# Attention values: the values stand in TensorE, placed by DMA, with repeated denominator columns, and a new step table

## What is computed

```python
q, k, v = heads(xn @ Wq.T + bq), heads(ctx @ Wk.T + bk), heads(ctx @ Wv.T + bv)
scores  = (q @ k.T * tau + delta) / sqrt(8)          # 512 x 77 for each head
x = x + softmax(scores) @ v -> merged heads @ Wo.T + bo
```

## Time and profile before

| | us |
|---|---|
| median of 3 runs | 204.74 (204.21 to 206.11) |
| profiled execution | 205.09 |
| span of its instructions | 203.3 |
| mean granted TensorE clock | 0.973 |
| busy: TensorE, VectorE, ScalarE, GpSimd | 174.1, 124.9, 90.3, 59.9 |

### The profile page before, as it was taken

The page is one execution under the profiler, slowest core; times in us unless marked ns, Lnnn a source line. Parts: engine busy times, 40 slices in busy tenths (PEclk is TensorE's granted clock), DMA queues, the critical chain, the costliest instruction groups (busy, mean ns, idle before and its releaser), DMA issues.

```text
span 203.3 us, 3835 instructions
## 1 busy us (share of the span) xinstructions
PE 174.1 (86%) x1176; PEld 142.2 (70%) x1177; DVE 124.9 (61%) x386; ACT 90.3 (44%) x216; POOL 59.9 (29%) x73
## 2 busy tenths in 40 slices
PE   7796899989999969598999999889688989989940
PEld 2435778979949945483896779765477979989930
DVE  2799967598743786984265975355478454544420
ACT  5490466344551443322239164151265557555620
POOL 8873030001305250020020002034205645646441
PEclk9998899999999996999999999999999999999996
DMA  6999980000000000000000000002801281100000
GB/s 207 289 334 380 487 365 29 0 0 3 2 0 3 0 0 0 2 3 0 0 0 3 0 0 0 3 28 79 261 32 54 74 266 31 31 6 9 27 14 2
DMA packets 9219, 15.37 MB, mean 76 GB/s; under 512 B 1578, under 2 KB 6069, under 8 KB 9136
## 3 DMA queue, kind: packets, MB, share of 16 engines
q1 hardware_dynamic: 7680, 13.00, 18.5%
q0 software_dynamic: 1088, 1.60, 2.4%
q10 hardware_dynamic: 432, 0.53, 0.8%
HBM read 13.53 MB, written 5.44 MB: 93 GB/s over the span
## 4 chain that ended last, share of the span: by engine, by line
PE 59%; DVE 24%; issue 5%; ACT 5%; POOL 2%; DMA 2%; DVEq 0%; ACTq 0%; POOLq 0%
PE scores L1108 12%; PE acc L1001 11%; PE acc L1119 8%; PE shared L957 4%; DVE QG L721 4%; PE shared L1062 4%; PE scores L982 3%; PE shared L937 3%; DVE stats L662 3%; PE shared L1048 3%; DVE XN L680 2%; PE shared L930 2%; PE shared L909 2%; DMA X<-in_x 2%; PE shared L1035 2%
## 5 line engine op out<-in xcount | busy, mean ns | idle before, releaser
L1001 PE MATMUL acc<-VP,P 123*128 123x128 f32 (+1 forms) x320 | 41.8, 276 | 0.6 <-ACT P L598 0.6
L1001 PEld LDWEIGHTS acc<-VP,P 123*128 123x128 f32 (+1 forms) x320 | 39.8, 191 | 2.8 <-ACT P L598 1.0
L598 ACT ACTIVATE P<-scores 123x512 f32<-123x512 f32 (+1 forms) x40 | 22.9, 595 | 26.3 <-PE scores L982 23.5
L638 ACT ACTIVATE HT<-scores,B 128x128 f32<-128x128 f32 x88 | 25.4, 376 | 14.3 <-PE scores L1108 10.4
L731 DVE TENSOR_REDUCE MR<-shared 128x4 f32<-128x308 f32 x64 | 26.9, 469 | 2.2 <-PE shared L957 2.0
L506 POOL TENSOR_TENSOR X<-X,ROWS 128x512 f32<-128x512 f32 x6 | 7.7, 1275 | 65.9 <-DVE XN L680 65.8
L520 POOL DMA_INDIRECT out<-XS,token x22 | 21.6, 982 | 18.2 <-DVE XS L867 10.6
L1108 PE MATMUL scores<-XST,HT 128*128 128x128 f32 x176 | 24.1, 280 | 3.3 <-ACT XST L631 2.7
L1108 PEld LDWEIGHTS scores<-XST,HT 128*128 128x128 f32 x176 | 21.4, 192 | 5.0 <-ACT XST L631 3.6
L1119 PE MATMUL acc<-W,HT 128*128 x176 | 23.2, 276 | 1.1 <-ACT HT L638 1.1
L957 PE MATMUL shared<-KG,QG 98*128 98x308 f32 x64 | 20.5, 376 | 4.3 <-DVE QG L721 3.4
(11 more groups left out here) (123 smaller groups left out, 252.0 us busy)
## 6 DMA issues: line engine op xcount, KB each, us to landing
W<-in_w SPq DMA_DIRECT2D x16, 256.0 KB, 8.6
slots<-in_empty SPq DMA_DIRECT2D x1, 2860.0 KB, 15.6
XS<-slots SPq DMA_DIRECT2D x2, 650.0 KB, 6.2
XS<-slots SPq DMA_DIRECT2D x2, 390.0 KB, 3.9
W<-in_ffn0w SPq DMA_DIRECT2D x1, 534.0 KB, 8.9
XS<-slots SPq DMA_DIRECT2D x2, 260.0 KB, 2.9
X<-in_x SPq DMA_DIRECT2D x2, 256.0 KB, 5.1
B<-in_b SPq DMA_DIRECT2D x1, 512.0 KB, 7.3
```

Source lines behind the costliest of these rows:

```text
L598: act.activation(P[0:w, n % NP], scores[n % 2][0:w, :], ACT.Exp).then_inc(probs_ready, 1)
L638: ins = act.activation(HG1[:, t % NHB, c], hidden[t % 2][:, c], ACT.Gelu_apprx_tanh, bias=B1[:, bass.ds(expert[t] * NF + k, 1)])
L1001: ins = pe.matmul(acc[qt // 2][:, c:c + VW], P[0:w, n % NP, 128 * qt:128 * qt + 128], VP[0:w, l, b, j, half], start=(t == 0 and qt % 2 == ...
```

## The change

The values are projected once for each layer, for both batches (`vp/0`, `vp/1`: two products of 77 x 128), and VectorE adds their bias while it copies them to a new tile `VS`. SyncE then copies them by DMA into `VP`, which GpSimd has set to zero before: for each batch 12 transfers (`HEADS`), one for each piece of a head's 77 rows that lies in one tile, of 15 to 77 rows with two times 8 columns. In `VP` the 64 value columns of a half stand in front of 64 columns of ones, where the mask is repeated 8 times for each head, so the denominators come out once for every value column.

In `pv` the values stand in TensorE and the 512 columns of probabilities stream through in one product; the result is transposed already, and each half has its own `acc` bank. The new step `rd` makes the reciprocal of the denominators on ScalarE as exp(-ln(d)), and `on` is one VectorE product for each half, straight into `OT`. The `ot` steps, their transposes and the 8 filler products in the last `ot` and `wo` are gone. The context is stored once. On SyncE's queue the first placing stands before the weights of layer 1's attention and of the first feed-forward part, the second before the rest of the weights. The table of steps is another one.

```diff
-VC = DK + 1
-VW = 128
+VW = 2 * HALF * DK
...
+HEADS = [(h, j, max(h * KEYS, STARTS[j]) - STARTS[j], max(h * KEYS, STARTS[j]) - h * KEYS,
+          min((h + 1) * KEYS, STARTS[j] + WIDTHS[j]) - max(h * KEYS, STARTS[j]))
+         for h in range(HALF) for j in range(NT)
+         if max(h * KEYS, STARTS[j]) < min((h + 1) * KEYS, STARTS[j] + WIDTHS[j])]
...
+R_BV = R_SB + E
+R_N = R_BV + 2 * D
...
-        one/1/1 pv/0/1/8 km/1/0 xt/2/0 pre/2/0 km/1/1 pv/0/1/9 on/0/1 q/1/0/0 max/1/0/0:2 ot/0/1 max/1/0/2:4 vp/1/1/1
...
+        ln/0/0 xn/0/0 kp/0 vp/0 xt/0/0 ks/0 q/0/0/0:2 km/0/0 max/0/0/0:6 one/0 max/0/0/6:8 ln/0/1 mt/0/0/0
+        max/0/0/8:11 sc/0/0/0:2 max/0/0/11 pre/0/0 max/0/0/12 xn/0/1 pv/0/0/0 max/0/0/13 pv/0/0/1 xt/0/1 sc/0/0/2
+        max/0/0/14:16 sc/0/0/3 q/0/1/0 mt/0/0/1 pv/0/0/2 sc/0/0/4 pv/0/0/3 q/0/1/1 pv/0/0/4 sc/0/0/5 km/0/1 sc/0/0/6
+        max/0/1/0:3 sc/0/0/7 pv/0/0/5 sc/0/0/8 max/0/1/3:6 pv/0/0/6 rd/0/0/0 max/0/1/6 sc/0/0/9 max/0/1/7 pv/0/0/7:9
+        on/0/0/0 pv/0/0/9 rd/0/0/1 mt/0/1/0 vp/1 pre/0/1 max/0/1/8 on/0/0/1 max/0/1/9:11 sc/0/1/0:2 max/0/1/11 wo/0/0
+        sc/0/1/2 ln/1/0 max/0/1/12:14 pv/0/1/0 xn/1/0 pv/0/1/1 sc/0/1/3 pv/0/1/2 max/0/1/14:16 sc/0/1/4 xt/1/0
+        pv/0/1/3 one/1 mt/0/1/1 gate/0 kp/1 sc/0/1/5 pv/0/1/4 rd/0/1/0 ut/0 pre/1/0 hid/0/0:4 sc/0/1/6 out/0 sc/0/1/7
+        pv/0/1/5 sc/0/1/8 ln/2/0 on/0/1/0 xn/2/0 sc/0/1/9 pv/0/1/6:8 ks/1 xt/2/0 q/1/0/0 pv/0/1/8:10 km/1/0
+        max/1/0/0:3 pre/2/0 max/1/0/3:5 rd/0/1/1 max/1/0/5 on/0/1/1 max/1/0/6:8 q/1/0/1 mt/1/0/0 wo/0/1 max/1/0/8
+        sc/1/0/0 km/1/1 ln/1/1 max/1/0/9 pv/1/0/0 xn/1/1 sc/1/0/1 max/1/0/10 sc/1/0/2 xt/1/1 max/1/0/11 sc/1/0/3
+        max/1/0/12:14 gate/1 pv/1/0/1:3 max/1/0/14 ut/1 max/1/0/15 sc/1/0/4 pre/1/1 hid/1/0:4 mt/1/0/1 out/1 sc/1/0/5
+        pv/1/0/3 sc/1/0/6 ln/2/1 pv/1/0/4 rd/1/0/0 xn/2/1 on/1/0/0 sc/1/0/7 pv/1/0/5 xt/2/1 sc/1/0/8 q/1/1/0:2
+        pv/1/0/6 sc/1/0/9 max/1/1/0 pv/1/0/7 max/1/1/1 pv/1/0/8 max/1/1/2:6 pv/1/0/9 max/1/1/6:11 rd/1/0/1 mt/1/1/0
+        on/1/0/1 max/1/1/11:14 sc/1/1/0:2 wo/1/0 sc/1/1/2 max/1/1/14 pre/2/1 max/1/1/15 pv/1/1/0 ln/3/0 pv/1/1/1
+        mt/1/1/1 sc/1/1/3 pv/1/1/2 sc/1/1/4:6 pv/1/1/3 sc/1/1/6 xn/3/0 xt/3/0 pv/1/1/4 route/0 sc/1/1/7:9 rd/1/1/0
+        pv/1/1/5 prob/0 rank/0 pv/1/1/6 tiles/0 sc/1/1/9 pv/1/1/7:9 on/1/1/0 pv/1/1/9 rd/1/1/1 on/1/1/1 wo/1/1 ln/3/1
+        xn/3/1 moe/-1 xt/3/1 moe/0 route/1 moe/1 prob/1 rank/1 tiles/1
...
+            def place_values(l):
+                sp.wait_ge(v_ready, l + 1)
+                sp.wait_ge(zeroed, 6 + l)
+                for b in range(B):
+                    for h, j, r, k, n in HEADS:
+                        o = VP[r:r + n, l, b, j, :, h * DK:(h + 1) * DK]
+                        v = VS[k:k + n, l, b].rearrange("p (s d) -> p s d", s=2)[:, :, h * DK:(h + 1) * DK]
+                        sp.dma_start(o, v).then_inc(v_placed[l][b], 16)
...
+            place_values(0)
+            sp.dma_start(ATT[1][:, :], att1).then_inc(in_att[1], 16)
             sp.dma_start(W0[:, :], ffn0w).then_inc(in_w0, 16)
             for i in range(3):
                 sp.dma_start(LB[32 * i:32 * i + 32, :], loraB).then_inc(in_lb, 16)
-            sp.dma_start(ATT[1][:, :], att1).then_inc(in_att[1], 16)
+            place_values(1)
...
-            finish(pool.memset(VP[:, :, :, :, :, HALF * VC:], 0.0), zeroed)
+            finish(pool.memset(VP[:, 0], 0.0), zeroed)
...
-            def ones_columns(l, b):
-                for half in range(2):
-                    o = VP[:, l, b, :, half, 0:HALF * VC].rearrange("p j (h c) -> p j h c", c=VC)[:, :, :, DK]
-                    finish(pool.tensor_copy(o, vm), ones_col)
+            def ones_columns(l):
+                m = vm.unsqueeze(3).to_broadcast([TW, NT, HALF, DK])
+                for b in range(B):
+                    for half in range(2):
+                        o = VP[:, l, b, :, half, HALF * DK:].rearrange("p j (h c) -> p j h c", c=DK)
+                        finish(pool.tensor_copy(o, m), ones_col)
...
+            finish(pool.memset(VP[:, 1], 0.0), zeroed)
...
-                    if n == 2 * B * 2 * NT - 1:
+                elif kind == "rd":
+                    _, l, b, half = s
+                    n = 2 * l + b
+                    act.wait_ge(probs_used, NT * (2 * n + half + 1))
+                    if n > 0:
+                        act.wait_ge(on_ready, 2 * (n - 1) + half + 1)
+                    act.activation(rden[:, half], acc[half][HALF * DK:, :], ACT.Ln).then_inc(act_chain, 1)
+                    chain += 1
+                    act.wait_ge(act_chain, chain)
+                    act.activation(rden[:, half], rden[:, half], ACT.Exp, scale=-1.0).then_inc(rden_ready, 1)
+                    if s[1:] == (1, B - 1, 1):
                         act.preload_act_table_set("gelu_apprx_tanh_and_others")
-                elif kind == "ot":
-                    _, l, b = s
-                    read(act, s)
-                    act.activation(OT[:, b], bank(s)[:, :], ACT.Identity, bias=ATT[l][:, A_BV:A_BV + 1]).then_inc(ot_ready, 1)
...
-                    _, l, b, j = s
+                    l = s[1]
                     read(dve, s)
-                    if (l, b, j) == (0, 0, 0):
-                        dve.wait_ge(in_con, 16)
-                    w = WIDTHS[j]
-                    o = VP[0:w, l, b, j, :, 0:HALF * VC].rearrange("p s (h c) -> p s h c", c=VC)[:, :, :, 0:DK]
-                    v = bank(s)[0:w, 0:D].rearrange("p (s h c) -> p s h c", s=2, c=DK)
-                    m = CON[0:w, C_VM + HALF * j:C_VM + HALF * (j + 1)].unsqueeze(1).unsqueeze(3).to_broadcast([w, 2, HALF, DK])
-                    dve.tensor_tensor(o, v, m, ALU.mult).then_inc(v_ready, 1)
+                    dve.wait_ge(in_rows, 16)
+                    bv = ROWS[0:KEYS, R_BV + D * l:R_BV + D * (l + 1)].unsqueeze(1).to_broadcast([KEYS, B, D])
+                    dve.tensor_tensor(VS[:, l], bank(s)[0:KEYS, 0:B * D].rearrange("p (b d) -> p b d", b=B), bv,
+                                      ALU.add).then_inc(v_ready, 1)
...
-                    _, l, b = s
-                    n = 2 * l + b
-                    dve.wait_ge(probs_used, 2 * NT * (n + 1))
-                    for i in range(2):
-                        o = acc[i][:, 0:4 * HALF * VC].rearrange("p (t h c) -> p t h c", t=2, c=VC)
-                        ins = dve.reciprocal(rden[:, b, 2 * i:2 * i + 2], o[:, :, :, DK])
-                    link(ins)
-                    for i in range(2):
-                        o = acc[i][:, 0:4 * HALF * VC].rearrange("p (t h c) -> p t h c", t=2, c=VC)
-                        rd = rden[:, b, 2 * i:2 * i + 2].unsqueeze(3).to_broadcast([128, 2, H, DK])
-                        dve.tensor_tensor(ON[:, b, 2 * i:2 * i + 2].rearrange("p t (h c) -> p t h c", c=DK),
-                                          o[:, :, :, 0:DK], rd, ALU.mult).then_inc(on_ready, 1)
+                    _, l, b, half = s
+                    dve.wait_ge(rden_ready, 2 * (2 * l + b) + half + 1)
+                    dve.tensor_tensor(OT[64 * half:64 * half + 64, b], acc[half][0:HALF * DK, :], rden[:, half],
+                                      ALU.mult).then_inc(on_ready, 1)
                 elif kind in ("wo", "out"):
                     b = s[-1]
                     st = 1 if kind == "out" else 2 * s[1]
...
-                    _, l, b, j = s
-                    if (b, j) == (0, 0):
-                        pe.wait_ge(in_att[l], 16)
-                        pe.wait_ge(in_ctx, 16)
+                    l = s[1]
+                    pe.wait_ge(in_att[l], 16)
+                    pe.wait_ge(in_ctx, 16)
                     hold(s)
-                    w, k0 = WIDTHS[j], STARTS[j] % KEYS
-                    pe.matmul(bank(s)[0:w, 0:D], CTX[:, b, k0:k0 + w], ATT[l][:, A_V:A_V + D],
-                              start=True, stop=True).then_inc(full[use[s][0]], 1)
+                    for b in range(B):
+                        ins = pe.matmul(bank(s)[0:KEYS, b * D:(b + 1) * D], CTX[:, b, :], ATT[l][:, A_V:A_V + D],
+                                        start=True, stop=True)
+                    ins.then_inc(full[use[s][0]], 1)
                 elif kind == "q":
                     _, l, b, pair = s
...
-                        pe.wait_ge(v_ready, NT * (B * l + b + 1))
-                        pe.wait_ge(zeroed, 6)
-                        pe.wait_ge(ones_col, 2 * (B * l + b + 1))
-                        if n > 0:
-                            pe.wait_ge(on_ready, 2 * nth["on", l, b])
+                        pe.wait_ge(v_placed[l][b], 16 * len(HEADS))
+                        pe.wait_ge(zeroed, 6 + l)
+                        pe.wait_ge(ones_col, 2 * B * (l + 1))
+                    if j == 0 and (l, b) != (0, 0):
+                        pe.wait_ge(on_ready, 2 * (2 * l + b - 1) + half + 1)
                     pe.wait_ge(probs_ready, n + 1)
-                    cols = HALF * VC
```

(42 more changed lines are left out.)

66 lines of the change are left out of this document (17 added, 49 removed).

## The result

The changed kernel takes 200.84 us (median of 4 runs, 200.54 to 201.5) against 204.48 for the kernel before beside it: ratio 0.985, interval 0.981 to 0.989. Two later measurements, on two chips, gave 0.974 [0.969, 0.979] and 0.983 [0.978, 0.988]. So the change is faster by 1.5 to 2.6%, 3.6 us in the first measurement, where 6.2 were forecast (204.74 to 198.5). The prices of most steps were as predicted; what they are worth together was not.

What follows compares the result with a forecast made beforehand. No single engine was taken as the bound: TensorE held 59% of the chain, VectorE 24%. Gains of 8.8 us less 2.2 charged made 6.6, from 205.09 to 198.5 us; range 194.5 to 203.8.

Steps and rivals of the forecast that it cites:

- Value products: Attention stretch: one product of 512 columns replaces four of 128, 0.86 instead of 0.89 us a step, 0.7 us gained.
- Value projection: Attention stretch: two steps replace twenty; 1.7 us gained before the first value product, 2.8 us after, together 4.5 us.
- Normalising: Between last value product and output projection: 0.8 us gained for the first batch, 0.5 for the third; ScalarE charged 2.2.
- rival (a): ScalarE and the order eat the gain: all 6.7 us of added ScalarE work on the path, 203.0 us; chance 0.12.
- Tail: From the last value product to the output projection: 2.2 us instead of 3.0, gain 0.8 us.
- New order: Layer 1, before its first maxima: two value steps fill TensorE's 1.6 us wait for the query split, 1.5 us gained.
- Placing and constants: SyncE's queue: batch 0 placed at 18.3 to 23.0 us, costed at nothing; constants landing late kept as 1.4 us in range.
- the threshold of 0.9: Cost in us of a placing transfer above which placing comes late; at 1.8 the kernel takes 209.4 us, chance 0.10.
- GpSimd: Zeroing and copying before the first value product: done at 16 us, 24.5 at the upper bound, hidden; range keeps 2 us.
- The clock and the part behind 146 us: Second feed-forward part, after the tail: not touched by the change, expected unchanged at 57 us.
- a sign of being wrong: Behind the tail: a second fall of the clock there would make the forecast wrong.
- rival (b): Leaner TensorE and unfilled tail meet the lower clock more often: three stretches return 5.2 of 6.6 us, 203.7; chance 0.08.

Runs made afterwards that it cites:

- stand_only: Kernel before with values standing, repeated denominator columns and ScalarE reciprocals; 20 masked projections and order kept, no placing, values' bias left out: ratio to before 1.023.
- placing_double: Changed kernel with each placing transfer cut in two, 48 instead of 24 per layer, same bytes: 208.96 us, ratio to the kernel before 1.024.
- values_once: Kernel before with values projected once per layer and placed by DMA, product form and order as before: 200.96 us against 200.23, ratio 1.004.
- third series: One chip: changed kernel again 200.51 us, with the old order from 100 us 206.02, old forms in the new order 212.48, placing_double 208.96.
- the square: Old or new forms crossed with old or new step order, ratios to the kernel before: old/old 1.004, new/old 1.022, old/new 1.036, both new 0.983.

## Why the prediction was right in sign and too large

1. **Value products:** right in price. A step is 0.86 us on the chain. The term, 0.7 us, is too small to be seen apart.
2. **Value projection, 4.5 us:** this step failed. The 8 records are there, but its form alone is worth nothing in the old order (1.004 [1.000, 1.007]; first expert product 1.1 us earlier in one execution). A share of the chain was taken for a saving. In the part before the first value product the term had 1.7 us, and 0.6 came, since VectorE's maxima hold the chain in the projections' place; then the longer fall of the clock took its share (two value steps in 3.59 us instead of 1.79). Where the remaining 2.8 us of the term went was not followed step by step.
3. **Normalising:** the prices were right (0.59 and 0.63 us on ScalarE, 0.68 on VectorE), the 1.3 us gained by the earlier batches not: in the old order the standing form costs 2.3% (stand_only). There rival (a) happens, and beyond its price: gains of 0.7 + 0.8 + 0.5 + 0.8 less 6.7 make 3.9 us slower, 4.9 were measured (205.12 - 200.23), the clock's share in it unknown.
4. **Tail:** right. The last value product ends at 131.44, the output projection starts at 133.60: 2.2 us. Before it was 3.0.
5. **New order, 1.5 us:** the wait is filled as predicted. But with the new forms the order from 100 us on is worth 5.1 to 5.5 us, over three times that, and the prediction did not price it: it read the table for one wait and not for when VectorE's maxima are fed.
6. **Placing and constants:** right. The addition ran at 8.71 us without a wait for the row constants; 24 transfers took 20.0 us, 0.83 each, under the threshold of 0.9. By 9.15 + 12 x 0.83 + 2.1 = 21.2 us, an estimate (2.1 is the small landing of the earlier trace rows), batch 0 was there 2.3 us before the first value product at 23.51, which was forecast for 22.5. The Trainium skill (SBUF — State Buffer, section The DMA setup-cost knee) puts a fixed price on every transfer and most of it in the completion. That fits the last of 24 in placing_double, which released TensorE 1.9 us after its issue began; with transfers back to back on one queue, though, the issue is what adds up, 0.78 us of SyncE for each in the median, and the completion counts once.
7. **GpSimd:** right, hidden. Zeroing takes 2.23 us twice, a copy 0.52 us in the mean, under the 0.8 taken.
8. **The clock and the part behind 146 us:** forecast at 57 us, now 58.0, with a third fall at 145 us, which the prediction had named as a sign of being wrong, and waits for the gathered tokens of up to 1.8 us ahead of it. Over ten executions such a fall goes with 1.8 us more, so rival (b) is the likeliest taker of that part of the shortfall. Its cause stays open: the fall near 145 us is there in two of the three profiles of the same changed kernel, so it can't be put down to the dropped fillers. Nor was the wait before the fall of 76 us its cause as far as can be seen: that wait is filled, and the fall came at 77 us as long as before, while `values_once` keeps the wait of 1.55 us and has no fall there. Over all executions the changed kernel has a mean clock of 0.954 in the third series, the kernel before 0.973. Within the kernel before, 0.01 of mean clock goes with 0.7 to 0.8 us; by that, an estimate and no proof of cause, the clock takes 1.3 to 1.5 of the 2.4 us that were missing in the profiled execution (6.6 forecast, 4.2 measured in the span).

So two errors of opposite sign met: 4.5 + 1.3 us of forms that bring little or nothing by themselves, and an order worth far more than 1.5 us. The terms are not additive, as the square shows. That the time still fell into the range from 194.5 to 203.8 is in part luck.

## What to carry to other kernels

Work that stands on the chain may have another engine's work just beneath it, which holds the chain as soon as it is gone: before counting it as saved, name what TensorE does in that place afterwards. In a kernel with a written order, form and order are one change; try the new form in the old table and the old form in the new one before crediting either. Many small DMAs on one queue are priced by the issue, 0.7 to 0.8 us each here, so count them and lay the sum against the first user and against all that is queued behind.
